# Layer 2 of a graph-attention stack: probabilities transposed in 32x32 blocks by VectorE and moved by DMA in groups of four tiles, instead of by TensorE

## The chip, the cores and the metric

The kernel runs on one core of one Trainium2 chip. The metric is the device time of one execution in microseconds. Engines are named PE (TensorE, the matrix engine; PEld is its weight load), DVE (VectorE), ACT (ScalarE), POOL (GpSimd) and SP (SyncE, which here only issues DMAs).

## What is computed

Input are 16 graphs of 1024 nodes with 64 features, and for each an adjacency matrix of 1024 x 1024 integers. Four attention layers follow one another, each as `x = layernorm(x + gnn(x, adj))`. Layer 2, which the change touches, has 8 heads:

```python
q, k, v = (x @ W + b for each)            # reshaped to 8 heads of 64
scores = einsum('bmhd,bnhd->bhmn', q, k) / sqrt(64) + edge_bias[edges]
scores = leaky_relu(scores, 0.2)
scores = where(edges > 0, scores, -1e9)
attn = softmax(scores, axis=-1)
out = einsum('bhmn,bnhd->bmhd', attn, v).reshape(b, m, 8 * 64)
return out @ Wp + bp
```

All is float32. The adjacency holds zeros and ones.

## The kernel before

The kernel loops over the 16 graphs. A tile is the block of 128 nodes (rows) by 1024 nodes (columns) of one head's attention matrix: layers 0, 1 and 3 have 8 tiles each, layer 2 has 64 (8 heads by 8 row blocks, taken as 4 pairs of heads). A step of layer 2 is the two tiles of a head pair for one row block, so layer 2 has 32 steps (`STEPS2`), eight per pair.

A tile n of layer 2 goes through these stations:

- PE, `scores`: a mask matmul (identity times mask, 2 instructions of 512 columns) and the query-key product as two float32r parts (q_hi, q_lo, 2 instructions each) into one of two PSUM slots, `score[n % 2]`. The slot is free when the leaky step of tile n-2 is done.
- ACT, `relu_part`: ReLU of the scores to `probs[n % 4]` in SBUF, line 668.
- DVE, `leaky`: combines scores and ReLU into the negated leaky ReLU with its row minimum, in place, line 926. (Another, longer branch is taken for graphs with more than one edge type.)
- ACT, `exps`: the exponential in place, with the row sum, line 679.
- PE, `turn_tile`: eight 128x128 transposes of `probs` into the PSUM area `turn`, line 384.
- DVE, `copy_tile`: copy of `turn` to `probsT[n % 4]` in SBUF, line 955.
- PE, `pv_pair`: the values product of the two tiles of a step, 8 x 2 matmuls of 128 columns (two instructions each, 32 in all), the two heads in two halves of the array's columns, into `outT`, line 412. It is done in two halves, `part` 0 and 1.

All engines have hand-written instruction orders. On PE a step s issues the scores of the first tile of step s+1, the extra work if there is any, half a values product of an earlier step, the transposes of the first tile, the scores of the second tile of step s+1, a half product again, and the transposes of the second tile. Extra work per pair of heads comes in set steps: the heads of the pair before are transposed back (`turn_out`, step 2 of a pair), the queries of the next pair (steps 3 and 4, line 456) and its values (step 5, `make_vw`, line 469). DVE does per step: leaky of n+2, copy of n, leaky of n+3, copy of n+1. ACT: exponential of n, ReLU of n+2, exponential of n+1, ReLU of n+3. `keep_clock` puts matmuls without a use where PE would idle between layers.

SP issues per graph the loads of x and of its transpose for the next graph, the eight 512 KB tiles of the next adjacency (`load_adj`; two buffers, each load from the third on waits until POOL has read the tile before, `s_adj_free`), and the store. POOL turns each adjacency tile into a mask (`convert`, lines 1177 to 1182), two per pair of heads, and between them adds the heads of each pair.

The semaphores that matter: `s_probs` (exponential done), `s_turned` and `s_turn_free` (`turn` filled and read), `s_pv` (values product done), `s_out_copied` (`outT` copied out by ACT).

Of the kernel before, what the change touches and what calls it, by code (L numbers as in the profile page):

```python
# [34 lines left out]
P = 128  # L35
# [17 lines left out]
PVS = NT // 2 * 2 + STEPS2 + NT  # L53
# [11 lines left out]
def extra_use(s):  # L65
# [7 lines left out]
    return None  # L73


def transposer_uses():
# [7 lines left out]
    for s in range(STEPS2):  # L84
        if extra_use(s):
            uses.append(extra_use(s))
        uses += [("tile", L2_0 + 2 * s), ("tile", L2_0 + 2 * s + 1)]
# [6 lines left out]
def build(nc, x, xT, adj, W0, W0T, a0T, W1, W1T, a1T, bias1, WqT, bq, WkT, bk, WvT, bv, edge_bias, Wp, bp,  # L94
# [3 lines left out]
    with ExitStack() as ctx:  # L98
# [90 lines left out]


# [22 lines left out]
        s_turned = sem("s_turned")  # L213
        s_turn_free = sem("s_turn_free")
# [45 lines left out]
        def _(sp):  # L260
# [9 lines left out]
            def load_adj(g, before):  # L270
                for t in range(NT):

                    if before is not None or t >= 2:
                        sp.wait_ge(s_adj_free, (0 if before is None else before * NT + NT) + t - 1)
                    sp.dma_start(adj_in[:, t % 2, :],
                                 adj[bass.ds(g, 1), t * P:(t + 1) * P, :].rearrange("a p j -> p (a j)")).then_inc(s_adj[t % 2], 16)

# [28 lines left out]
            load_adj(0, None)  # L306
            with sp.Fori(0, B - 1) as g:

                sp.wait_ge(s_xin_free, g + 1)
                load_x(g + 1)  # L310
                load_adj(g + 1, g)
# [3 lines left out]
            load_x(B - 1)  # L315
            store(B - 1)
# [6 lines left out]
        def _(pe):  # L323
# [75 lines left out]
            def pv_pair(g, s, part):  # L399

                pair, t = divmod(s, NT)
                n = L2_0 + 2 * s
                if part == 0:
                    if t == 0:
                        in_sbuf(pe, g, ("vw", pair))
                        pe.wait_ge(s_out_copied, g * 14 + 4 + 2 * pair)
                    if s == 0:
                        side_in_sbuf(pe, g, ("beta", 0))
                    in_sbuf(pe, g, ("tile", n + 1))
# [109 lines left out]
            with pe.Fori(0, B) as g:  # L519
# [31 lines left out]
                for s in range(STEPS2):  # L551
# [4 lines left out]
                    late = s >= 2 and t != 1  # L556
# [16 lines left out]
                    if s:  # L573
                        pv_pair(g, s - 1, 0)
                        if t == 0:
                            pv_pair(g, s - 1, 1)
# [694 lines left out]
```

## Time and profile before

| quantity | value |
|---|---|
| median of 3 runs | 10149.99 us (10137.19 to 10156.25) |
| span of the profiled execution | 10161.5 us |
| PE busy | 9662.1 us (95%) |
| DVE busy | 7780.4 us (77%) |
| ACT busy | 6859.0 us (67%) |
| POOL busy | 1409.9 us (14%) |
| mean granted PE clock | 0.988 of full |
| DMA traffic | 95.11 MB |

The profiled execution's own time is its span; the runs' times are taken without the profiler. Times in rows are microseconds from the span's start; a merged row gives start, duration, engine, line, operation, output and input, and the number of instructions. Matmuls are pipelined and their ends are modelled, so consecutive PE rows overlap by a little, and the distance of two starts is the better measure.

### The profile page before, as it was taken

The page shows a single profiled execution, that of the slowest core. Times are in us where ns is not written, and L with a number is a line of the kernel's source. Part 1 is how long each engine was busy: PE and PEld are TensorE (multiplying, and loading weights), DVE is VectorE, ACT ScalarE, POOL GpSimd, SP SyncE. Part 2 cuts the span into 40 slices and gives each one's busy share as a digit, 9 for nine tenths or more (in the row PEclk, how much of TensorE's full clock was granted, in tenths as well). Part 3 has the DMA queues.
Part 4 walks back from the last instruction along what each step waited for, and adds up shares of the span by engine and source line. Part 5 has one row for each costly group of instructions (what it writes and reads, how often), then busy time and mean ns, then how long its engine had stood idle before and what let it go on. Part 6 is the DMA issues. An engine that isn't in the chain of part 4 may idle for free.

```text
span 10161.5 us, 205999 instructions
## 1 busy us (share of the span) xinstructions
PE 9662.1 (95%) x80620; PEld 5343.6 (53%) x80620; DVE 7780.4 (77%) x11658; ACT 6859.0 (67%) x7901; POOL 1409.9 (14%) x582
## 2 busy tenths in 40 slices
PE   7999999999999999999999999999999999999999
PEld 5537355373554735547365473654736446364463
DVE  5786967869678696786967869687696876968769
ACT  4676756768567685766857668576685766857667
POOL 1203012030110301103011020111201112021000
PEclk9999999999999999999999999999999999999999
DMA  1000000000000000000000000000000000000000
GB/s 33 10 9 14 1 13 9 9 14 1 15 7 9 14 1 17 5 9 14 1 17 6 9 14 1 17 5 13 10 1 17 5 13 10 2 19 3 5 1 2
DMA packets 60304, 95.11 MB, mean 9 GB/s; under 512 B 41794, under 2 KB 41794, under 8 KB 59266
## 3 DMA queue, kind: packets, MB, share of 16 engines
q1 hardware_dynamic: 59266, 80.98, 2.6%
q8 instruction: 687, 11.26, 0.5%
q14 instruction: 351, 2.88, 0.1%
HBM read 76.77 MB, written 4.19 MB: 8 GB/s over the span
## 4 chain that ended last, share of the span: by engine, by line
issue 55%; PE 34%; DVE 4%; POOL 4%; ACT 3%; DVEq 0%; SPq 0%; POOLq 0%; DMA 0%; ACTq 0%
PE psum L384 9%; PE psum L376 8%; PE psum L412 5%; PE psum L372 4%; PE psum L456 3%; PE psum L616 2%; ACT work L668 2%; DVE work L955 2%; PE psum L469 1%; DVE q_lo L1019 1%; POOL no_edge L1179 1%; ACT q_hi L716 1%; POOL rstd L1199 1%; POOL mask_next L1182 1%; PE psum L448 1%
## 5 line engine op out<-in xcount | busy, mean ns | idle before, releaser
L825 ACT ACTIVATE work<-vw,ucol 128x1024 f32<-128x1024 f32 x3072 | 3313.8, 1141 | 484.5 <-PE psum L616 482.2
L616 PE MATMUL psum<-work,pick 128*32 128x512 f32 x32768 | 3634.7, 596 | 4.1 <-ACT work L825 3.7
L1126 DVE TENSOR_SCALAR work<-vw,ucol 128x1024 f32<-128x1024 f32 x5120 | 3446.8, 749 | 209.9 <-ACT ucol L805 116.3
L926 DVE CUSTOM_DVE_ANT_0 work<-psum,work 128x1024 f32<-128x1024 f32 x1284 | 1568.5, 1223 | 888.8 <-ACT work L668 840.1
L616 PEld LDWEIGHTS psum<-work,pick 128*32 128x32 f32 x32768 | 1014.7, 110 | 2330.3 <-issue 2229.6
L955 DVE COPY work<-psum 128x1024 f32<-128x1024 f32 x1410 | 1723.1, 1222 | 653.4 <-PE psum L384 649.0
L668 ACT ACTIVATE work<-psum,beta 128x1024 f32<-128x1024 f32 x1024 | 1142.0, 1115 | 1180.6 <-PE psum L376 1180.6
L384 PE MATMUL psum<-ident,work 128*128 128x128 f32 x11280 | 1555.7, 281 | 237.1 <-DVE work L955 95.9
L384 PEld LDWEIGHTS psum<-ident,work 128*128 128x128 f32 x11280 | 1222.6, 142 | 667.2 <-issue 505.9
L679 ACT ACTIVATE work<-work,least 128x1024 f32<-128x1024 f32 x1282 | 1463.5, 1142 | 38.9 <-DVE least L926 38.4
L412 PE MATMUL psum<-work,vw 128*64 128x128 f32 x16384 | 1064.0, 277 | 4.7 <-DVE work L955 4.7
L412 PEld LDWEIGHTS psum<-work,vw 128*64 128x64 f32 x16384 | 878.5, 137 | 291.5 <-issue 277.2
L1199 POOL TENSOR_TENSOR rstd<-rstd,neg_half 128x8 f32<-128x8 f32 x64 | 124.0, 1938 | 5480.9 <-DVE rstd L1000 5480.9
L372 PE MATMUL psum<-mask,ident_b 128*128 128x512 bf16 x2568 | 787.2, 389 | 98.9 <-issue 42.7
L376 PE MATMUL psum<-x_split,q_hi 128*128 128x512 f32 x2048 | 840.0, 491 | 0.0
L376 PE MATMUL psum<-x_split,q_lo 128*128 128x512 f32 x2048 | 646.7, 397 | 0.0
L448 PE MATMUL psum<-mask,ident_b 128*128 128x512 bf16 x2112 | 476.6, 380 | 0.0
L1210 POOL TENSOR_TENSOR za<-za,heads_T 128x512 f32<-128x512 f32 x96 | 122.8, 1279 | 2513.4 <-DVE heads_T L962 2509.6
L376 PEld LDWEIGHTS psum<-x_split,q_hi 128*128 128x128 f32 x2048 | 391.9, 191 | 149.4 <-issue 2.8
L668 ACT ACTIVATE work<-psum,sbias 128x1024 f32<-128x1024 f32 x260 | 287.6, 1112 | 251.7 <-PE psum L376 251.7
L394 PE MATMUL psum<-work,vw 128*64 128x128 f32 x6144 | 437.0, 286 | 20.4 <-DVE work L955 19.9
L394 PEld LDWEIGHTS psum<-work,vw 128*64 128x64 f32 x6144 | 341.7, 141 | 199.6 <-issue 151.0
(130 smaller groups left out, 6240.2 us busy)
## 6 DMA issues: line engine op xcount, KB each, us to landing
adj_in<-in_adj SPq DMA_DIRECT2D x128, 512.0 KB, 3.5
x_in<-in_x SPq DMA_DIRECT2D x17, 256.0 KB, 3.2
xT_in<-in_xT SPq DMA_DIRECT2D x17, 256.0 KB, 4.5
out<-yout SPq DMA_DIRECT2D x16, 256.0 KB, 2.6
work<-in_WqT SPq DMA_DIRECT2D x1, 128.0 KB
work<-in_WkT SPq DMA_DIRECT2D x1, 128.0 KB
work<-in_WvT SPq DMA_DIRECT2D x1, 128.0 KB
work<-in_Wp SPq DMA_DIRECT2D x1, 128.0 KB
```

The costliest lines, as they stand in the source:

```text
L372: pe.matmul(slot[:, cols], ident_b[:], mask[:, t, cols], start=True, stop=False)
L376: mm = pe.matmul(slot[:, cols], left, right[:, cols], start=False, stop=(k == len(parts) - 1))
L384: mm = pe.transpose(turn[:, j * P:(j + 1) * P], src[:, j * P:(j + 1) * P], ident[:])
L394: mm = pe.matmul(outT[half, t * P:(t + 1) * P], value[:, j, :], src[:, j * P:(j + 1) * P], start=(j < 2), stop=(j >= NT - 2))
L412: mm = pe.matmul(outT[F * h:F * h + F, t * P:(t + 1) * P], vw[:, pair % 2, j, F * h:F * h + F], probsT[(n + h) % 4][:, j * P:(j + 1) * P], ...
L616: mm = pe.matmul(slot[32 * q:32 * q + 32, cols], pick[:, 15 - kk:47 - kk], ring[kk % 4][q][:, cols], start=False, stop=(kk == 15), skip_gr ...
L668: act.activation(probs[n % 4], score[n % 2], ACT.Relu, bias=bias, scale=GAIN[layer]).then_inc(s_relu, 1)
L679: act.activation(probs[n % 4], probs[n % 4], ACT.Exp, bias=least[:, n % 4:n % 4 + 1], scale=-1.0, accum_out=total).then_inc(s_probs, 1)
L825: ins = act.activation(ring[kk % 4][q], v3, ACT.Relu, bias=col)
L926: dve.tensor_tensor_reduce(probs[n % 4], score[n % 2], probs[n % 4], -ALPHA[layer], 3.0e38, ALU.add, ALU.min, least[:, n % 4:n % 4 + 1]).t ...
L955: dve.tensor_copy(probsT[k], turn).then_inc(s_turn_free, 1)
L1126: ins = dve.tensor_scalar(ring[kk % 4][q], v3, col, 0.0, ALU.add, ALU.max)
```

## The change

- VectorE transposes a tile in 32x32 blocks straight from `probs` in SBUF to a group buffer `blocks[k % 2]` in SBUF (four tiles, 16 KB per partition). This leaves each block turned, but not moved to its partitions.
- A group ("quad") k is the four tiles of steps 2k and 2k+1. When its four tiles are written, SP issues 16 DMAs from `blocks` to `quadT`, each of 32 partitions, 8 runs, 512 B per run, which put block row a to block column c. `MOVED` is 15: groups 0 to 14 of 16 go this way, the last is transposed by PE as before.
- The values product takes a whole group: 256 columns per matmul, 8 x 2 matmuls, half of it in each step, `LAG` = 2 groups behind the scores.
- The next graph's adjacency loads 2 to 7 are issued between the groups' DMAs, and POOL converts 3, 3, 2 and 0 tiles in the four pairs instead of 2 each.
- Heads are transposed back in step 6 of the next pair, and `outT` is copied in two halves in steps 0 and 4.
- ScalarE's ReLU waits for VectorE's block transpose of tile n-4 in place of PE's transpose.
- Scratch of the branch for more edge types is placed elsewhere, as its buffers are now used.

```diff
+QUADS = STEPS2 // 2
+MOVED = QUADS - 1
+LAG = 2
+PV2 = NT // 2 * 2
+PVS = PV2 + QUADS + NT
...
-    if t == 2 and pair:
+    if t == 6 and pair:
         return ("heads", pair - 1)
...
+        blocks = [quad_of(8), quad_of(12)]
+        quadT = [quad_of(4), quad_of(16)]
...
+            ADJ_AFTER = {2: (2,), 3: (3,), 4: (4,), 8: (5,), 10: (6,), 11: (7,)}
+
+            def move_quads(g, more):
+
+                for k in range(MOVED):
+                    written = sp.to_reg(g * 4 * MOVED + 4 * k + 4)
+                    read = sp.to_reg(ONE + g * PVS + PV2 + k - 1) if k >= 2 else None
+                    sp.wait_ge(s_setup, SETUP)
+                    sp.wait_ge(s_blocks, written)
+                    if k >= 2:
+                        sp.wait_ge(s_pv, read)
+                    src = blocks[k % 2].rearrange("p (b c x) -> p b c x", c=4, x=P)
+                    dst = quadT[k % 2].rearrange("p (b c x) -> p b c x", c=4, x=P)
+                    for turn_ in range(4):
+                        for a in range(4):
+                            c = (a + turn_) % 4
+                            sp.dma_start(dst[32 * c:32 * c + 32, :, a, :], src[32 * a:32 * a + 32, :, c, :])\
+                              .then_inc(s_moved[k % 4], 16)
+                    if more:
+                        load_adj(g + 1, g, ADJ_AFTER.get(k, ()))
...
+            def pv_quad(g, k, part):
+
+                pair, tt = divmod(k, 4)
                 if part == 0:
-                    if t == 0:
+                    if tt == 0:
                         in_sbuf(pe, g, ("vw", pair))
...
+                    if k < MOVED:
+                        pe.wait_ge(s_moved[k % 4], g * (MOVES[k % 4] * 256) + (moved_before(k) + 1) * 256)
+                    else:
+                        in_sbuf(pe, g, ("tile", L2_0 + 4 * k + 3))
+                src = turned_quad(k).rearrange("p (b a h x) -> p b a h x", a=4, h=2, x=F)
+                cols = slice(2 * tt * P, 2 * tt * P + 2 * P)
                 for j in range(part * NT // 2, (part + 1) * NT // 2):
                     for h in range(2):
-                        mm = pe.matmul(outT[F * h:F * h + F, t * P:(t + 1) * P], vw[:, pair % 2, j, F * h:F * h + F],
-                                       probsT[(n + h) % 4][:, j * P:(j + 1) * P], start=(j == 0), stop=(j == NT - 1))
+                        dst = outT[F * h:F * h + F, cols].rearrange("p (t a i) -> p a t i", t=2, a=4)
+                        mm = pe.matmul(dst, vw[:, pair % 2, j, F * h:F * h + F],
+                                       src[:, j, :, h, :].rearrange("p a (t i) -> p a t i", t=2),
+                                       start=(j == 0), stop=(j == NT - 1))
...
-                    if late:
-                        pv_pair(g, s - 2, 1)
-                    if not extra:
+                    if s >= 2 * LAG:
+                        pv_quad(g, s // 2 - LAG, s % 2)
+                    if not in_quad(n)[3]:
                         turn_tile(g, n)
-                        if more:
-                            scores(g, n + 3)
...
+                    if more:
+                        scores(g, n + 3)
+                    if not in_quad(n)[3]:
+                        turn_tile(g, n + 1)
+                for k in range(QUADS - LAG, QUADS):
+                    pv_quad(g, k, 0)
+                    pv_quad(g, k, 1)
...
+                if n - 4 >= L2_0 and in_quad(n - 4)[3]:
+                    act.wait_ge(s_blocks, g * 4 * MOVED + n - 4 - L2_0 + 1)
...
+            def turn_tile(g, n):
+
+                k, half, h, moved = in_quad(n)
+                if k >= 2 and half == 0 and h == 0:
+                    dve.wait_ge(s_moved[(k - 2) % 4],
+                                g * (MOVES[(k - 2) % 4] * 256) + (moved_before(k - 2) + 1) * 256)
+                if moved:
+                    dve.wait_ge(s_probs, ONE + g * TILES + n + 1)
+                    dst = blocks[k % 2].rearrange("p (b h t i) -> p b h t i", h=2, t=2, i=32)
+                    dve.transpose(dst[:, :, h, half, :], probs[n % 4].rearrange("p (b j) -> p b j", j=32))\
+                       .then_inc(s_blocks, 1)
+                    return
...
-                    copy_tile(g, n)
-                    if more and not extra:
+                    turn_tile(g, n)
+                    if more:
                         leaky(g, n + 3, flagged)
-                    copy_tile(g, n + 1)
-                    if more and extra:
-                        leaky(g, n + 3, flagged)
+                    turn_tile(g, n + 1)
...
-                        for t in (2 * pair, 2 * pair + 1):
+                        for t in ((0, 1, 2), (3, 4, 5), (6, 7), ())[pair]:
```

## Rows read from the trace of the kernel before

**Rows 1.** Timeline of PE: start, us, engine, line, operation; layer 2's beginning and end.
```profile
3322.61 1.01 PE L372 MATMUL psum<-mask,ident_b 128*128 128x512 bf16 x2
...
3327.92 0.67 PE L372 MATMUL psum<-mask,ident_b 128*128 128x512 bf16 x2
...
3573.62 1.14 PE L422 MATMUL psum<-ident,heads_T 128*128 128x128 f32 x8 [0.70 <-ACT heads_T L696]
```

**Rows 2.** Busy time of a window inside layer 2: PE, PEld, DVE, ACT, POOL, clock, DMA.
```profile
3388.00:3451.00 63.00, 61.43 (x518) 46.35 (x516) 42.07 (x52) 40.20 (x54) 21.37 (x8) 1.00 0.05 18
```

**Rows 3.** Timeline of PE, a steady tile of layer 2.
```profile
3443.36 1.09 PE L412 MATMUL psum<-work,vw 128*64 128x128 f32 x16
3444.39 1.09 PE L384 MATMUL psum<-ident,work 128*128 128x128 f32 x8
3445.32 0.59 PE L372 MATMUL psum<-mask,ident_b 128*128 128x512 bf16 x2
...
3446.77 1.09 PE L412 MATMUL psum<-work,vw 128*64 128x128 f32 x16
```

**Rows 4.** Timeline of DVE and ACT in steady tiles, with idle time before.
```profile
3452.70 1.22 DVE L955 COPY work<-psum 128x1024 f32<-128x1024 f32 x1
3454.97 1.23 DVE L926 CUSTOM_DVE_ANT_0 work<-psum,work 128x1024 f32<-128x1024 f32 x1 [1.04 <-ACT work L668]
...
3453.71 1.12 ACT L668 ACTIVATE work<-psum,beta 128x1024 f32<-128x1024 f32 x1 [1.17 <-PE psum L376]
```

**Rows 5.** Groups by line, 3325 to 3572: busy, mean ns, idle before and its releaser.
```profile
L955 DVE COPY work<-psum 128x1024 f32<-128x1024 f32 x64 | 78.2, 1222 | 35.4 <-PE psum L384 35.4
L668 ACT ACTIVATE work<-psum,beta 128x1024 f32<-128x1024 f32 x64 | 71.4, 1115 | 75.3 <-PE psum L376 75.3
```

**Rows 6.** Timeline of PE: a whole values product of two tiles, and what follows.
```profile
3394.14 1.97 PE L412 MATMUL psum<-work,vw 128*64 128x128 f32 x32
3396.03 1.09 PE L384 MATMUL psum<-ident,work 128*128 128x128 f32 x8
```

**Rows 7.** The page's costliest groups: layer 3's DVE operation from SBUF to SBUF.
```profile
L1126 DVE TENSOR_SCALAR work<-vw,ucol 128x1024 f32<-128x1024 f32 x5120 | 3446.8, 749 | 209.9 <-ACT ucol L805 116.3
```

**Rows 8.** SP issues: start and us in the timeline; ns min/median/max by line.
```profile
4.55 0.65 SPq L264 DMA_DIRECT2D work<-in_WqT  x1
...
L267 SPq DMA_DIRECT2D x_in<-in_x x17: 383/384/434, 15.3 to 9549.1; - x17
...
L268 SPq DMA_DIRECT2D xT_in<-in_xT x17: 532/547/591, 15.8 to 9549.5; - x17
```

**Rows 9.** The page's DMA issues: count, KB each, us from issue to landing.
```profile
xT_in<-in_xT SPq DMA_DIRECT2D x17, 256.0 KB, 4.5
out<-yout SPq DMA_DIRECT2D x16, 256.0 KB, 2.6
```

**Rows 10.** Windows of the store and of an adjacency load: last columns are DMA share, GB/s.
```profile
3234.00:3238.50 4.50, 3.90 (x28) 3.01 (x28) 1.87 (x3) 1.96 (x4) 0.00 (x0) 0.79 0.27 62
...
3263.00:3264.00 1.00, 0.02 (x1) 0.05 (x2) 0.59 (x2) 0.00 (x0) 0.38 (x1) 1.00 0.99 356
```

**Rows 11.** Groups by line: the longest operation of POOL's convert, three per tile.
```profile
L1177 POOL TENSOR_SCALAR mask_next<-adj_in 128x1024 bf16<-128x1024 int32 x120 | 436.5, 3638 | 16.2 <-POOL mask_next L1182 11.2
```

**Rows 12.** Timeline of PE: the extra work of a pair, queries and values.
```profile
3412.57 1.98 PE L456 MATMUL psum<-xTa,Aq 65*128 65x512 f32 x4
...
3431.21 2.05 PE L469 MATMUL psum<-Cv,xTa 65*128 65x128 f32 x16
```

**Rows 13.** Windows of 3.4 us: after the length PE busy; the third last is the clock.
```profile
3224.90:3228.30 3.40, 1.26 (x9) 0.86 (x8) 3.13 (x7) 2.69 (x4) 0.00 (x0) 1.00 0.04 10
3228.30:3231.70 3.40, 1.50 (x4) 0.81 (x4) 3.26 (x19) 0.60 (x2) 1.42 (x1) 0.62 0.02 5
3332.00:3335.40 3.40, 2.25 (x15) 1.62 (x14) 3.12 (x6) 2.58 (x5) 1.86 (x1) 1.00 0.45 154
3335.40:3338.80 3.40, 3.21 (x18) 2.16 (x17) 2.17 (x4) 2.24 (x3) 0.00 (x0) 1.00 0.00 0
```

More of the change, by code:

```diff
@@ L73, in extra_use, with in_quad, moved_before @@
     return None
+def in_quad(n):
+    s, h = divmod(n - L2_0, 2)
+    k, half = divmod(s, 2)
+    return k, half, h, k < MOVED
+def moved_before(k):
+    return len(range(k % 4, k, 4))
+MOVES = tuple(len(range(r, MOVED, 4)) for r in range(4))
 def transposer_uses():
@@ L86, in transposer_uses @@
             uses.append(extra_use(s))
-        uses += [("tile", L2_0 + 2 * s), ("tile", L2_0 + 2 * s + 1)]
+        uses += [("tile", n) for n in (L2_0 + 2 * s, L2_0 + 2 * s + 1) if not in_quad(n)[3]]
     uses += [("heads", HP - 1), ("xT", 2), ("v3", 0)]
@@ L188, in build, with quad_of, turned_quad @@
         v3 = vw[:, 0, :, :].rearrange("p a b -> p (a b)")
+        def quad_of(first):
+            return work[:, first:first + 4, :].rearrange("p a b -> p (a b)")
+        blocks = [quad_of(8), quad_of(12)]
+        quadT = [quad_of(4), quad_of(16)]
+        def turned_quad(k):
+            return quadT[k % 2] if k < MOVED else blocks[k % 2]
         s_load = sem("s_load")
@@ L213, in build @@
         s_turned = sem("s_turned")
+        s_blocks = sem("s_blocks")
+        s_moved = [sem(f"s_moved{i}") for i in range(4)]
         s_turn_free = sem("s_turn_free")
@@ L315, in _ @@
             load_x(B - 1)
+            move_quads(B - 1, False)
             store(B - 1)
@@ L555, in _ @@
                     extra = extra_use(s)
-                    late = s >= 2 and t != 1
                     if more:
@@ L795, in _ @@
                     if t == 0 and pair:
-                        copy_out(g, 1 + pair, NT + s)
-                copy_out(g, 1 + HP, NT + STEPS2)
+                        copy_out(g, 1 + pair, PV2 + 4 * pair - 2, (0,))
+                    if t == 4 and pair:
+                        copy_out(g, 1 + pair, PV2 + 4 * pair, (1,))
+                copy_out(g, 1 + HP, PV2 + QUADS - 2, (0,))
+                copy_out(g, 1 + HP, PV2 + QUADS, (1,))
                 x_turned(g, 2)
@@ L932, in leaky @@
                 head = 2 * pair + h
-                scaled, part = work[:, 8, :], work[:, 9, :]
+                scaled, part = probs[n % 4], zb[:].rearrange("p t f -> p (t f)")
                 ready = dve.to_reg(g * L3_0 + n + 1)
@@ L938, in leaky @@
                 for k in range(2, TYPES):
-                    typed(dve.tensor_scalar(part, mask[:, t, :], k * CODE, delta[:, k, head:head + 1], ALU.is_equal,
-                                            ALU.mult))
-                    typed(dve.tensor_tensor(scaled, scaled, part, ALU.add))
-                typed(dve.scalar_tensor_tensor(out=part, in0=scaled, scalar=ALPHA[2], in1=scaled, op0=ALU.mult,
+                    for cols in (slice(0, HALF), slice(HALF, N)):
+                        typed(dve.tensor_scalar(part, mask[:, t, cols], k * CODE, delta[:, k, head:head + 1],
+                                                ALU.is_equal, ALU.mult))
+                        typed(dve.tensor_tensor(scaled[:, cols], scaled[:, cols], part, ALU.add))
+                typed(dve.scalar_tensor_tensor(out=scaled, in0=scaled, scalar=ALPHA[2], in1=scaled, op0=ALU.mult,
                                                op1=ALU.max))
-                dve.tensor_tensor_reduce(probs[n % 4], part, part, -0.5 / GAIN[2], 3.0e38, ALU.add, ALU.min,
+                dve.tensor_tensor_reduce(scaled, scaled, scaled, -0.5 / GAIN[2], 3.0e38, ALU.add, ALU.min,
                                          least[:, n % 4:n % 4 + 1]).then_inc(s_leaky, 1)
+            def turn_tile(g, n):
[9 more added lines that the diff above has]
+                    return
+                filled(g, ("tile", n))
+                dst = turned_quad(k).rearrange("p (b a h t i) -> p b a h t i", a=4, h=2, t=2, i=32)
+                dve.tensor_copy(dst[:, :, :, h, half, :], turn.rearrange("p (b a i) -> p b a i", a=4, i=32))\
+                   .then_inc(s_turn_free, 1)
             def copy_tile(g, n):
```

51 lines of the change are left out of this document (21 added, 30 removed).

## The prediction, made before the changed kernel was built or run

> **What bounds the kernel now.** I read the stages of one graph first (busy time per window), then TensorE's timeline inside layer 2, then the same stretch on VectorE and ScalarE, then the waits grouped by line. One graph takes about 635 us (the span over 16). Layer 2 runs from its first scores at 3322.61 to the transpose of the last pair's heads at 3573.62, 251.0 us [rows 1]. In its middle the windows show PE busy 61.4 of 63 us, VectorE 42.1, ScalarE 40.2 [rows 2]: TensorE bounds this stage. A steady tile repeats every 3.41 us on PE (3443.36 to 3446.77): values product 1.03, eight transposes 0.93, scores 1.45, with no idle mark [rows 3]. VectorE spends 1.15 on the leaky step and 1.15 on the copy out of PSUM (start to start), then idles 1.04; ScalarE idles 1.17 [rows 4]. Over the stage the idle time of both ends on TensorE's scores or transposes [rows 5]. So taking transposes off PE can shorten this stage, and only this stage; the other 384 us of a graph stay as they are.
>
> **What goes.** 60 of 64 tiles per graph lose their PE transposes: 60 x 0.93 = 56 us of PE time per graph, 893 us in all. The last group of four keeps them. The values product keeps its columns: 4 x 0.95 = 3.8 us per group of four tiles (32 instructions in 1.90 us per two tiles [rows 6]); 256 columns per matmul instead of 128 halve the instruction count. I bound that between -1.9 us (if the time went by instruction) and, for the strided source and the 32-column runs in PSUM, +3.8 (each column at half pace), and take 0: source and result keep contiguous runs of 64 and 32 values.
>
> **What comes on VectorE.** A 32x32-block transpose of 128x1024 from SBUF to SBUF in place of the copy from PSUM. No row has it. Bounds: 0.75 us (the fastest SBUF to SBUF 1024-column operation [rows 7]) to 2.3 (two passes of the copy). I take the copy's 1.15, the nearest in columns and type. VectorE then needs 2.3 per tile, 9.2 per group of four, below what follows.
>
> **What comes on SP and the DMA queues.** Each of 15 groups per graph issues 16 DMAs of 128 KB (32 partitions x 8 runs of 512 B), 3840 in all, on SP alone. Issue price: the 128-partition x load, the one with most runs, costs 0.38 us, loads on 64 partitions 0.55 to 0.65 [rows 8]. The new ones have 32 partitions, so I go by the latter, 0.66 from start to start (bounds 0.43 and 0.9: the 128-partition price, and one more step as large as that from 128 to 64). Landing: 2.6 for the store and 4.5 for a read of 256 KB [rows 9]; for 128 KB inside SBUF I take 2.4 (1.8 to 4). From the last block written to a usable group: D = 0.1 + 15 x 0.66 + 2.4 = 12.4 us. Transfers: the store ran 256 B packets at share 0.27 and 62 GB/s, so about 230 GB/s if always busy; the adjacency reads about 356 at share 0.99 [rows 10]. A group's 2.1 MB takes 6 to 9 us at that, under the 10.6 of issue, so it adds nothing here.
> The Trainium skill (SBUF — State Buffer, "Door 1: The DMA port swizzle") speaks against this: how many of the 16 ports the partitions reach sets the bandwidth, and 32 adjacent partitions reach 8. No row here shows it; an estimate by that page's 436 GB/s halved is 9.6 us a group, still under the issue time, but without the margin.
> SP's other work: the adjacency loads of the next graph are put behind groups 2, 3, 4, 8, 10 and 11. Each waits for GpSimd, whose convert is three operations, the longest 3.6 us [rows 11]; by the schedule below each awaited convert is over before its load's turn, so I cost them at nothing (behind a late one all later moves would queue, 16 at a time). Register moves ahead of the waits run while SP is idle.
>
> **The cycle.** Group k is multiplied in steps 2k+4 and 2k+5 (a step is two tiles). Let E be PE's end of step 2k+1. The last tile's path behind it is ReLU 1.1, leaky 1.15, transpose 1.15 and handoffs: blocks complete at E + 3.5. They land at E + 3.5 + D. From there PE does half a product 1.9, scores 1.46, scores 1.46, the other half 1.9, scores 1.46 = 8.2 us, and that ends step 2k+5, two groups later. So two periods are 3.5 + D + 8.2, P = (D + 11.7)/2 = 12.05 us, against PE's own work of 4 x 1.46 + 3.8 = 9.65: the waits on the DMAs, about 2.4 us per group, take the place of the wait on TensorE. Before, four tiles took 13.65 plus the extras.
>
> **Sum for one graph.** Fill: the first scores to the end of the two starting tiles stay 5.3 us [rows 1]; steps 0 to 3 have no product and go at VectorE's 4.6 plus handoffs, 4.9 each, plus 1.2 for the query split in step 3: 20.8. Group 0's blocks are ready at 5.3 + 9.8 + 3.5 = 18.6, landed at 31.0, and PE is there at 26.1 + 3.4 = 29.5: wait 1.5. Then 13 periods (steps 4 to 29) at 12.05: 156.7. Extras (queries 1.9, values 2.0 [rows 12], heads 1.0, eight transposes like a tile's): those in even steps lie inside the wait; five in odd steps count half, 4.9. Clock: 3.4 us with PE busy for only 1.26 were followed by a granted clock of 0.62, 3.4 us with 2.25 busy by 1.00 [rows 13]. The waits of 2.4 lie between; 3.4 us at the 1.2 GHz level instead of 2.4 cost 1.7, and I count 0.5 per group, 6.5. Tail: from step 30 on 3.5 + D + 7.6 for the two last groups + 0.7 = 24.2; this part was short before because only one and a half pairs were left. Total 26.1 + 1.5 + 156.7 + 4.9 + 6.5 + 24.2 = 219.9, against 251.0: 31.1 us less per graph, 498 us in 16. The profiled execution's span is 10161.5, the median 10149.99, 0.1% apart; the saving is 4.9% of either, and from the median it gives 9652 us.
> D counts 6.5 times in the 13 periods, once in the tail and once in the first wait: each us of D is 8.5 us per graph, 136 us in all. At D = 16 nothing is left.
>
> **Rivals.**
> (a) Cheap issue: at 0.43, D = 0.1 + 6.45 + 2.2 = 8.8, and PE's work bounds again, with extras 11.1 per group: 26.1 + 144.3 + 20.5 = 191, 60 us per graph less, 9190 us. For it: the 128-partition rows. Against it: the 64-partition ones. 0.15.
> (b) Slower than before: the 16 DMAs of a group take 17 us to land, by an issue price of 0.9 or because a 32-partition transfer runs at half the rate of [rows 10], 115 to 178 GB/s, 12 to 18 us per group. Then P = 14.35, and 26.1 + 6 + 13 x (14.35 + 1.4) + 28.7 = 266, 15 us per graph more, 10,380 us. It decides from D = 16. For it: many packets of 512 B, no such transfer in the trace. 0.22.
> (c) The clock: if each wait drops it and a group's 8.2 us of PE work behind it lose 1.7 us or more, P grows by about 1.2 beyond what is counted: 13 x 1.2 = 15.6, half of the gain given back, 9900 us. 0.15.
> (d) The strided product at half pace: PE's work per group 13.4, P = 13.95, + 31 per graph: about 10,150 us, no change. 0.08, shared by the same and the slower side.
> By the Trainium skill (SBUF — State Buffer, the note on cachelines under "Door 1: The DMA port swizzle") any non-contiguous PSUM pattern slows matmuls much; that is rival (d). Runs of 32 values here are contiguous, and no row shows such a pattern.
> (e) Forecast: waits of some 2 us per group on the moved blocks, 0.40. That the change does not take effect can nearly be excluded: the trace has no instruction of the branch for flagged graphs, and the unflagged one turns 60 tiles as described.
>
> **Numbers.** 9652 us. The range takes in (a) nearly and (b) up to its own price: 9230 to 10,350, with about 0.08 left out below and 0.12 above. About 0.2% (20 us) is what a measurement of this kernel can tell from no change. Faster by more: 0.40 + 0.15 + 0.15 = 0.70; same 0.06; slower 0.24.
>
> **What would show it.** In layer 2's steady stretch PE should show idle time before the product, released by the moved DMAs, of 1 to 4 us per group, a group every 12 to 13 us; SP's 16 issues should span about 10 us; VectorE's transpose 1.2 us. No idle before the product and a group per 11 us is (a); a group per 15 or more is (b), and issue durations against landing times tell which half; granted clock under 0.9 through layer 2 is (c); product instructions of twice the length are (d). Most likely to be wrong: the issue price, then the landing.

## The result and the profile after

The changed kernel takes 9713.61 us (9705.1 to 9722.03) against 10151.01 for the kernel before on the same chip: ratio 0.9568, 95% interval 0.9554 to 0.9581. The forecast was 9652 in a range of 9230 to 10,350. 437 us were saved where 498 were expected. One execution of all those below, of the kernel with four moves on ScalarE's queue, was in a slow state (14,790.52 us at a granted clock of 0.553, against 10,025 to 10,041 for its other three), and it counts in that kernel's median alone.

The page of after (engine, busy us, share, instructions; the moving queue; the chain that ended last; groups by line; landing):

```profile
PE 8693.8 (90%) x64203; PEld 4229.6 (44%) x64748; DVE 7718.4 (79%) x11658; ACT 6774.4 (70%) x7901; POOL 1410.6 (15%) x582
...
q1 hardware_dynamic: 1103746, 584.54, 25.5%
...
issue 59%; PE 16%; SPq 11%; DVE 5%; ACT 4%; DMA 3%; POOL 2%; DVEq 0%; ACTq 0%; POOLq 0%
...
L477 PE MATMUL psum<-work,vw 128*64 128x256 f32 x8192 | 1105.8, 419 | 403.9 <-DMA work<-work 403.7
L1020 DVE STREAM_TRANSPOSE work<-work 128x1024 f32<-128x1024 f32 x960 | 1190.5, 1240 | 40.0 <-DMA work<-work 38.9
...
work<-work SPq DMA_DIRECT2D x3840, 128.0 KB, 2.4
```

PE lost 968 us of busy time, but 404 us came back as idle time before the values product (L477), nearly all of it released by the moved DMAs. Nothing of that kind stood on the page of before. SP's queue, at 0% of the chain of work that ended last before, is now 11% of it. VectorE's busy time hardly changed: 960 block transposes took the place of 960 copies. 404 us are 1.7 a group, within the 1 to 4 that the forecast had named as its sign.

PE's timeline in the same graph as [rows 1]: layer 2's first scores, the first half products of groups 0 to 4, the last of the 16 groups, the transpose of the heads. The bracket is the idle time before the row and what ended it.

```profile
3171.11 0.59 PE L431 MATMUL psum<-mask,ident_b 128*128 128x512 bf16 x2
...
3199.69 2.70 PE L477 MATMUL psum<-work,vw 128*64 128x256 f32 x16 [3.42 <-DMA work<-work]
...
3212.51 1.95 PE L477 MATMUL psum<-work,vw 128*64 128x256 f32 x16
...
3227.30 3.68 PE L477 MATMUL psum<-work,vw 128*64 128x256 f32 x16 [4.97 <-DMA work<-work]
...
3240.15 1.95 PE L477 MATMUL psum<-work,vw 128*64 128x256 f32 x16 [0.37 <-DMA work<-work]
...
3387.90 8.81 PE L477 MATMUL psum<-work,vw 128*64 128x256 f32 x64 [2.55 <-DMA work<-work]
...
3396.64 1.41 PE L488 MATMUL psum<-ident,heads_T 128*128 128x128 f32 x8
```

Layer 2 takes 3396.64 - 3171.11 = 225.5 us against 251.0; one graph earlier it is 222.0 (2570.56 to 2792.54) against 250.2. So 25.5 and 28.2 us saved, and the spans (10161.5 and 9713.2) give 28.0 a graph on average. Outside layer 2, from the heads' transpose to the next layer 2, the time moved from 380.4 to 379.5 us: the change lives in the stage where it was put. The span is 225.5 = 28.6 to the first product, 173.1 for 13 groups (13.3 each, from 3199.69 to group 13's 3372.79), 23.85 for the rest.

The timeline of SP's queue, the moves of three groups and more (start, time over all issues, count):

```profile
3187.35 38.09 SPq L328 DMA_DIRECT2D work<-work  x48
3225.77 0.34 SPq L309 DMA_DIRECT2D adj_in<-in_adj  x1
3226.32 10.95 SPq L328 DMA_DIRECT2D work<-work  x16
3237.58 0.34 SPq L309 DMA_DIRECT2D adj_in<-in_adj  x1
3241.70 10.49 SPq L328 DMA_DIRECT2D work<-work  x16
...
3332.33 11.60 SPq L328 DMA_DIRECT2D work<-work  x16
```

The sixteen issues of a group begin when VectorE has written its last block, at 3241.70, and the product of that group starts at 3253.98: D = 12.3 us. The adjacency load behind a group costs SP 0.34 us. Below, D is compared between kernels as (time of a group's issues) - (one issue) + (median landing): here 10.49 - 0.62 + 2.4 = 12.3.

That is the D of the groups with an even number. In those with an odd one, an issue among the fourth to seventh takes about 1 us longer, so that the sixteen take 11.3 to 11.7 us on average (10.95 and 11.60 in the rows above). From the first issue to the last landing, all 240 groups average 12.8. It is so with half of the bytes too (10.3 and 10.9 to 11.5), so full transfers are not the reason. Of the 122 issues in after that take over 0.25 us more than the median, 115 have a 16 KB packet of the queue that the page names instruction (q8) between 1.5 us before and 0.2 us after them, with half of the bytes 111 of 112; of the 3718 other issues in after it is 158. In the group that starts at 3253.75 the fifth issue takes 1.55 us, and the DMA queues from 3253.7 to 3258.2 show:

```profile
q8 instruction: 1, 0.02, 1.4%
```

That is a coincidence in time; no run here changes it, so that the packet is the cause is not shown.

### The profile page after: what moved, and what is told of

Its sections match the earlier page's. It is cut to its first block, busy times and chain, and to the rows that moved or that the text cites. A ratio compares the mean times of both kernels' runs of the same rounds, so it can differ in the third digit from the quotient of the medians.

```text
span 9713.2 us, 176082 instructions
## 1 busy us (share of the span) xinstructions
PE 8693.8 (90%) x64203; PEld 4229.6 (44%) x64748; DVE 7718.4 (79%) x11658; ACT 6774.4 (70%) x7901; POOL 1410.6 (15%) x582
## 3 DMA queue, kind: packets, MB, share of 16 engines
q1 hardware_dynamic: 1103746, 584.54, 25.5%
## 4 chain that ended last, share of the span: by engine, by line
issue 59%; PE 16%; SPq 11%; DVE 5%; ACT 4%; DMA 3%; POOL 2%; DVEq 0%; ACTq 0%; POOLq 0%
SPq L328 11%; PE psum L477 4%; PE psum L435 3%; DMA work<-work 3%; ACT work L728 2%; DVE work L1020 2%; PE psum L674 2%; PE psum L431 2%; DVE work L989 1%; PE psum L522 1%; PE psum L443 1%; POOL rstd L1279 1%; ACT work L739 1%; PE psum L514 1%; PE psum L453 1%
## 5 line engine op out<-in xcount | busy, mean ns | idle before, releaser
L674 PE MATMUL psum<-work,pick 128*32 128x512 f32 x32768 | 3623.5, 594 | 12.1 <-ACT work L888 12.1
L477 PE MATMUL psum<-work,vw 128*64 128x256 f32 x8192 | 1105.8, 419 | 403.9 <-DMA work<-work 403.7
L1020 DVE STREAM_TRANSPOSE work<-work 128x1024 f32<-128x1024 f32 x960 | 1190.5, 1240 | 40.0 <-DMA work<-work 38.9
L477 PEld LDWEIGHTS psum<-work,vw 128*64 128x64 f32 x8192 | 617.0, 148 | 841.7 <-issue 364.6
L431 PE MATMUL psum<-mask,ident_b 128*128 128x512 bf16 x2231 | 734.5, 400 | 261.5 <-DVE least L989 164.6
L435 PE MATMUL psum<-x_split,q_hi 128*128 128x512 f32 x2048 | 855.3, 499 | 0.0
L443 PE MATMUL psum<-ident,work 128*128 128x128 f32 x3600 | 500.0, 283 | 167.6 <-ACT work L739 80.9
L435 PE MATMUL psum<-x_split,q_lo 128*128 128x512 f32 x2048 | 648.4, 398 | 0.0
L1257 POOL TENSOR_SCALAR mask_next<-adj_in 128x1024 bf16<-128x1024 int32 x120 | 436.5, 3638 | 1164.5 <-DMA adj_in<-in_adj 1156.4
L443 PEld LDWEIGHTS psum<-ident,work 128*128 128x128 f32 x3600 | 393.1, 142 | 362.3 <-issue 305.4
L1037 DVE COPY work<-psum 128x1024 f32<-128x1024 f32 x386 | 470.8, 1220 | 84.6 <-PE psum L443 81.5
L435 PEld LDWEIGHTS psum<-x_split,q_hi 128*128 128x128 f32 x2048 | 403.5, 197 | 161.2 <-issue 18.7
L514 PE MATMUL psum<-mask,ident_b 128*128 128x512 bf16 x2032 | 459.5, 380 | 6.3 <-issue 3.0
L453 PE MATMUL psum<-work,vw 128*64 128x128 f32 x6144 | 434.6, 285 | 29.3 <-DVE work L1037 29.3
```

The source lines that it names most:

```text
L431: pe.matmul(slot[:, cols], ident_b[:], mask[:, t, cols], start=True, stop=False)
L435: mm = pe.matmul(slot[:, cols], left, right[:, cols], start=False, stop=(k == len(parts) - 1))
L443: mm = pe.transpose(turn[:, j * P:(j + 1) * P], src[:, j * P:(j + 1) * P], ident[:])
L477: mm = pe.matmul(dst, vw[:, pair % 2, j, F * h:F * h + F], src[:, j, :, h, :].rearrange("p a (t i) -> p a t i", t=2), start=(j == 0), stop ...
L674: mm = pe.matmul(slot[32 * q:32 * q + 32, cols], pick[:, 15 - kk:47 - kk], ring[kk % 4][q][:, cols], start=False, stop=(kk == 15), skip_gr ...
L1020: dve.transpose(dst[:, :, h, half, :], probs[n % 4].rearrange("p (b j) -> p b j", j=32))\
```

## The experiments

Ratios are to the kernel before, on the same chip. Two questions were open: what in the moves sets D (the count of issues, their bytes, or the partitions they reach), and what else is on the path. The expectations call some kernels by short names: e3 has 8 DMAs over 64 partitions, e5 the new order on VectorE, e6 and e7 that order and 2 or 4 moves on ScalarE's queue.

**Half of the bytes, half of the DMAs.**

```diff
# half of the bytes
-dst[32 * c:32 * c + 32, :, a, :], src[32 * a:32 * a + 32, :, c, :]
+dst[32 * c:32 * c + 32, 0:4, a, :], src[32 * a:32 * a + 32, 0:4, c, :]
# half of the DMAs
-for turn_ in range(4):
+for turn_ in range(2):
```

> The changed kernel with its 16 DMAs per group each moving 4 of the 8 runs, so 64 KB instead of 128 KB (half of the moved probabilities stay behind, so layer 2's output is not the reference's). Theory: a group's time from written to usable, D, is 16 issues of 0.66 us on SP's queue plus one landing of 2.4; bytes don't count. Then nothing moves: 9700 us within 30, 16 issues still span 10 to 10.6 us. Rival, transfers: if D is set by the bytes or by 32 partitions reaching few ports, D falls from 12.3 towards 7 and the time to about 9150 us.

> The changed kernel with only the first 8 of a group's 16 DMAs (the other half of the blocks is not moved, so layer 2's output is not the reference's). Theory: D falls to 0.1 + 7 x 0.66 + 2.4 = 7.1 us, under the 7.6 at which TensorE's own work fills the period; the wait before the product vanishes, a group takes 11.1 us with extras instead of 13.3, the granted clock in layer 2 rises to 0.98 or more, layer 2 takes about 189 us instead of 225.5, and the kernel about 9130 us (9080 to 9250). Rival: if something else of the new order holds the groups at 13 us (VectorE's order, ScalarE, the product's strided operands), it stays above 9500.

Half of the bytes: 9661.43 (0.9507, 0.9488 to 0.9526), 52 us less than after. Half of the DMAs: 9204.21 (0.9057, 0.9039 to 0.9075), 509 less. The line of the moves with half of the bytes (ns min/median/max of an issue, then us to landing):

```profile
L328 SPq DMA_DIRECT2D work<-work x3840: 585/601/2137, 182.0 to 9351.5; - x192
...
DMA to landing us min/median/max: 2.0/2.0/4.0
```

The same line with half of the DMAs, and who waited for them:

```profile
L328 SPq DMA_DIRECT2D work<-work x1920: 585/617/1928, 181.5 to 8885.6; - x192
...
  PEld psum L477: 11.2, 29
  PE psum L477: 0.2, 1
...
DMA to landing us min/median/max: 2.3/2.4/3.9
```

An issue costs the same, 0.60 to 0.62 us, with 64 KB as with 128 KB. With eight DMAs a group, PE no longer waits for them (0.2 us in the run), and what is left is near the forecast's rival (a), 9190, which stood for PE's own work being the bound. The forecast gave each us of D a price of 136 us. Half of the bytes lowers D by 0.6 (table below), which is 84 us by that price; 52 came, and 9661 is 39 below the expectation's 9700, which allowed 30.

**Half of the DMAs, all of the bytes, over 64 and then 128 partitions.** The count falls to 8, of 256 KB each.

```diff
# 64 partitions, turn_ in range(4), a in range(2)
-dst[32 * c:32 * c + 32, :, a, :], src[32 * a:32 * a + 32, :, c, :]
+dst[64 * c:64 * c + 64, :, 2 * (turn_ // 2) + a, :], src[64 * a:64 * a + 64, :, 2 * (turn_ // 2) + c, :]
# 128 partitions, turn_ in range(2), a in range(4)
-dst[32 * c:32 * c + 32, :, a, :], src[32 * a:32 * a + 32, :, c, :]
+dst[:, 4 * turn_:4 * turn_ + 4, a, :], src[:, 4 * turn_:4 * turn_ + 4, a, :]
```

> The changed kernel with 8 DMAs of 64 partitions and 256 KB per group in place of 16 of 32 partitions and 128 KB: the same bytes, half the issues (blocks land at the wrong partitions, so layer 2's output is not the reference's). Theory, count of issues: as with half the DMAs, 9130 us plus up to 60 for a landing 0.4 us longer. Rival, bytes: D stays above 11 and the time near 9650.

> Eight DMAs a group instead of sixteen, each of all 128 partitions and four runs (256 KB each), so that the bytes of a group stay as they are, 2.1 MB, and the count is halved as with eight DMAs of 64 partitions (9694.8). The blocks stay on their own partitions, so the products read rows in the wrong place and the output is not the reference's; what is computed, and how much, is the same. Theory A (the count of issues sets the step, and with it a second limit that belongs to moving 32 or 64 adjacent partitions, 35.9 to 42.7 ns a packet against 29.2 over 128): the issue stays near 0.65 us, the last of 8 is issued after 5.2 us and landed after about 8, so D falls from 12.3 to about 8 us, as with half of the DMAs (9204), and the run comes to 9200 to 9350. Theory B (the queue takes a time per byte or per row of the descriptor, whatever its shape): the issue grows to about 1 to 1.3 us, 8 issues span 8 to 10.5 us as with 64 partitions, and the run stays at 9650 to 9720.

64 partitions: 9694.84 (0.954, 0.9521 to 0.9559), a plain miss: halving the count gave 19 us. 128 partitions: 9295.15 (0.9156, 0.9139 to 0.9174), 418 less than after. The line of the moves over 64 partitions:

```profile
L328 SPq DMA_DIRECT2D work<-work x1920: 590/993/2502, 179.6 to 9392.3; - x192
...
DMA to landing us min/median/max: 3.2/5.0/9.0
```

The line of the eight moves over 128 partitions:

```profile
L327 SPq DMA_DIRECT2D work<-work x1920: 593/692/1710, 180.8 to 8977.9; - x192
...
DMA to landing us min/median/max: 2.6/3.6/4.8
```

Over 64 partitions the queue itself slows: 0.99 us an issue, and 5.0 to land, and a group's issues take 8.54 and 7.84 us in two groups, 8.2 on average, so that D = 8.2 - 1.0 + 5.0 = 12.2 is where it was. Over 128 the same bytes by the same count need 6.31 - 0.69 + 3.6 = 9.2, where theory A had about 8. So there is a second limit behind the count of issues, and it goes by partitions. A rival would be that the moves over 128 leave every byte on its partition, while the others cross. But of the eight over 64 half stay too (`c` equal to `a`), and they land no closer behind the one before (1.23 to 1.31 us, medians by place in the group) than those that cross (1.18 to 1.30); over 128 it is 0.88 to 0.93.

**Sixteen DMAs over 128 partitions; the order of the halves.** The first keeps count and bytes and changes only the partitions (`dst[:, 2 * turn_:2 * turn_ + 2, a, :]`); the second sends a in the order 0, 2, 1, 3.

> The changed kernel with its 16 DMAs of 128 KB per group each over all 128 partitions with 2 runs of 512 B, in place of 32 partitions with 8 runs: same bytes, same number of runs and DMAs (nothing changes partition, so layer 2's output is not the reference's). Theory A, partitions: 32 or 64 adjacent partitions reach only part of SBUF's ports, which held e3 at about 10 us for 2.1 MB and stretched the issues of e7; over 128 partitions the transfers take 7 us or less, and the issue costs 0.40 to 0.45 as in the loads on 128 partitions; D falls to about 9 and the time to 9200 us (9130 to 9300). Theory B, packets: 4096 runs of 512 B per group take that time by themselves whatever the partitions; landing and D stay at 11 or more, and the time at 9600 or more.

> The changed kernel with the source groups of a turn in the order 0, 2, 1, 3 in place of 0, 1, 2, 3, so that neighbours in the queue read and write different halves of the 128 partitions; nothing else. Theory A (ports): neighbouring DMAs overlap better, landing falls from 2.4 and the stretched issues (up to 2.1 us) get rarer: 20 to 80 us less than 9714. Theory B (packets), or engines that never run two DMAs at once: the same within 15.

9697.69 (0.9545, 0.9525 to 0.9566) and 9717.43 (0.9563, 0.9546 to 0.958): neither is worth anything alone, and both intervals overlap that of after. The first has the time of theory B without its reason: the same packets went faster in the kernel with 8 DMAs over 128 partitions, and what held this one was the issue, 0.62 us and not the 0.40 to 0.45 of the expectation. What the engines move shows in windows of some us while a group moves (the last two columns are the DMA share and GB/s; a share over 1 is more than one packet in flight). The windows are chosen so that no bytes of an adjacency load, which would count, fall into them. After, 16 DMAs over 32 partitions:

```profile
3243.00:3251.00 8.00, 7.84 (x40) 4.57 (x40) 6.72 (x8) 6.25 (x8) 0.00 (x0) 1.00 0.87 198
```

8 DMAs over 64 partitions:

```profile
3250.00:3258.00 8.00, 7.84 (x37) 4.50 (x37) 6.83 (x9) 6.85 (x11) 0.00 (x0) 1.00 1.12 219
```

8 DMAs over 128 partitions:

```profile
3104.00:3110.00 6.00, 6.00 (x32) 3.39 (x32) 5.49 (x8) 5.29 (x7) 0.00 (x0) 1.00 1.01 287
```

16 DMAs over 128 partitions:

```profile
3252.50:3261.00 8.50, 8.50 (x41) 4.99 (x41) 7.04 (x9) 7.12 (x9) 0.00 (x0) 1.00 0.68 196
```

The first and the last are the pace of the issues (131,072 B each 0.66 us are 198 GB/s), at 0.87 and 0.68 of the engines' time. At a full share the first would move 228, an estimate; two queues that push over 32 partitions reached 203 to 207 (below). Eight DMAs over 64 partitions move 219 with the engines full, eight over 128 move 287. A group's 2.1 MB then needs 9.2 to 10.3 us over 32 partitions, 9.6 over 64 and 7.3 over 128. Sixteen issues need 10.5. So after stands at two limits that nearly coincide: the issues bound it, and the transfers would just below. Taking one away alone (8 DMAs of 64 partitions; 16 of 128) gives 16 to 19 us, no more than the noise can hide; taking both gives 418. These runs follow roughly from D, at 136 us per us away from after's 12.27, half of the bytes with 32 us between:

| kernel | D | by D | measured |
|---|---|---|---|
| after | 12.3 | - | 9713.6 |
| half of the bytes | 10.25 - 0.60 + 2.0 = 11.65 | 9629 | 9661.4 |
| 8 of 64 partitions | 8.2 - 1.0 + 5.0 = 12.2 | 9704 | 9694.8 |
| 16 of 128 partitions | 10.56 - 0.62 + 2.2 = 12.1 | 9696 | 9697.7 |
| 8 of 128 partitions | 6.31 - 0.69 + 3.6 = 9.2 | 9299 | 9295.2 |
| half of the DMAs | 5.21 - 0.62 + 2.4 = 7.0 | 8996 | 9204.2 |

The last is beyond the point at which D stops to count, since PE's work is then the longer; by the same line its 9204 us would belong to a D of 8.5. With the averages of all groups in place of the D above (12.8 for after; 12.1, 12.7, 12.6, 9.5 and 7.2 in the table's order) the picture is the same.

**The clock.** Eight matmuls without a use stand before the product's wait, once the score slot is free.

```diff
+if k < MOVED and k < QUADS - LAG:
+    slot_free(g, L2_0 + 4 * (k + LAG) + 3)
+    for _ in range(KEEP_QUAD):
+        pe.matmul(score[1][:, 0:HALF], ident_b[:], mask[:, 0, 0:HALF], start=True, stop=True)
```

> The changed kernel with eight more matmuls without a use (0.22 us each, 1.8 us together) on TensorE before it waits for a moved group. Theory: part of what the prediction missed is the granted clock, 0.92 to 0.96 in layer 2, which falls to the 1.2 GHz level after the longer waits (a half product then took 3.68 us instead of 1.95). With the wait partly filled the clock stays at 0.98 or more there and the period loses 0.4 to 0.7 us: 9590 us (9550 to 9650). Rival: the filling delays the groups whose wait is shorter than 1.8 us by as much as the clock gives back: 9700 within 30, or slower.

9729.95 (0.9573, 0.9557 to 0.9589): no gain, though the mean granted clock rose from 0.972 to 0.988. Its timeline shows why this can't decide what the clock costs:

```profile
3235.11 1.90 PE L472 MATMUL psum<-mask,ident_b 128*128 128x512 bf16 x8 [0.90 <-DVE least L994]
3236.93 1.95 PE L482 MATMUL psum<-work,vw 128*64 128x256 f32 x16
```

The half product runs at full pace (1.95 instead of 3.68) without a wait of its own, but 1.8 us of filler stand before it and themselves wait for VectorE. What the products got back, the filler took. How much PE time the clock cost in after can be read from the products, the same 8192 instructions in each kernel. Busy us and mean ns with half of the DMAs, where PE hardly waits:

```profile
L477 PE MATMUL psum<-work,vw 128*64 128x256 f32 x8192 | 987.8, 385 | 0.4 <-DMA work<-work 0.2
```

After has 1105.8 us there, 118 more; with the filler it is 991.2. What those 118 us are worth in the run's time stays open.

**VectorE's order.** The block transpose of tile n+1 is placed ahead of the leaky step of n+3.

```diff
 turn_tile(g, n)
+early = in_quad(n)[3]
+if early:
+    turn_tile(g, n + 1)
 if more:
     leaky(g, n + 3, flagged)
-turn_tile(g, n + 1)
+if not early:
+    turn_tile(g, n + 1)
```

> The changed kernel with one edit on VectorE: in every step of a moved group the block transpose of tile n+1 comes ahead of the leaky step of tile n+3, so a group is complete right after its last exponential and not 3.5 us behind TensorE's end of the step. Theory: the period is half of (path to the last block + D + TensorE's 8.2 and its lost clock); taking 3.3 us from the path takes 1.65 from each of 13 periods until the next limit, SP's 16 issues and the adjacency load (about 11.1 us) or TensorE's work with extras (11.1). 9350 us (9280 to 9450). Rival: the period is already bound by a throughput, SP's issues or the transfers, and the chain only looks like it: then no gain over 20 us, 9690 or more. Second rival: the leaky step comes later, TensorE's slots are freed later, and it gets slower than 9714.

9508.09 (0.9359, 0.9344 to 0.9375): 206 us less than after, though 158 above the expectation. In after the last transpose of a group queues behind leaky steps with which VectorE catches up after it idled 5.47 us:

```profile
3233.99 1.22 DVE L989 CUSTOM_DVE_ANT_0 work<-psum,work 128x1024 f32<-128x1024 f32 x1 [5.47 <-ACT work L728]
...
3239.28 1.19 DVE L989 CUSTOM_DVE_ANT_0 work<-psum,work 128x1024 f32<-128x1024 f32 x1
...
3240.39 1.24 DVE L1020 STREAM_TRANSPOSE work<-work 128x1024 f32<-128x1024 f32 x1
```

One leaky step, 1.1 us, leaves the path of two periods. Part of the gain is also the clock's, as the waits got shorter: the products, 1105.8 us in after, are busy 70 us less:

```profile
L477 PE MATMUL psum<-work,vw 128*64 128x256 f32 x8192 | 1036.1, 399 | 255.0 <-DMA work<-work 254.8
```

The rest of the hoped gain was largely stopped by SP's queue. Over these four groups, 11.5 us each, it waits for VectorE for 1.9 us in all (SP's timeline; in four groups of after from 3253.75 it waited 7.1):

```profile
3183.31 46.06 SPq L328 DMA_DIRECT2D work<-work  x64
```

**Some of the moves on ScalarE's queue.** On top of that order, the last 2, then the last 4, of each 16 DMAs are issued by ScalarE (`ON_ACT`), between the exponential and the ReLU; then the four with the order 0, 2, 1, 3.

> As e5, and the last 2 of a group's 16 DMAs issued by ScalarE, behind its exponential of the next even step. Theory: SP's issues fall from 10.6 to 9.2 us, D by up to 1.3; if issue is what holds e5, 9250 to 9330; if the transfers hold it (2.1 MB took about 10 us with half the issues in e3), no gain beyond 30 us over e5. Rival: ScalarE's 1.2 us per group in front of its ReLU delay the scores' slots, and it is slower than e5.

> As e6 with 4 of the 16 DMAs on ScalarE: SP's issues fall to 7.9 us, ScalarE's work per group rises by 2.5 to about 12.5 with its extras. If issue bounds e5 and e6, another 50 to 100 us less than e6; if transfers bound, the same as e6 within 30; if ScalarE's queue bounds, slower than e6 by 100 or more.

> e7 (two issuing queues, block transposes first) with the order 0, 2, 1, 3. In e7 SP's 12 issues took 10.3 us instead of 7.9, so the transfers held both queues. Theory A: with neighbours on different halves the 12 issues take 8 to 9 us and the time falls by 200 us or more, to 9800 or less. Theory B: no change from 10037 within 40.

Two: 9406.88 (0.9261, 0.9246 to 0.9277), the fastest kernel here that does the whole work. Four: 10,036.53 (0.9877, 0.9857 to 0.9897), 630 slower than two. Four in the other order: 9928.36 (0.9772, 0.975 to 0.9794), 108 less. The kernel with two gained 101 us, between what its expectation gave for issues (9250 to 9330) and for transfers (at most 30), which fits that both held it. SP's timeline in the kernel with four:

```profile
3331.13 10.20 SPq L331 DMA_DIRECT2D work<-work  x12
```

ScalarE's in the same stretch, its own issues (ACTq) among its work:

```profile
3331.17 0.59 ACTq L760 DMA_DIRECT2D work<-work  x1
3331.32 0.19 ACT L742 ACTIVATION_READ_ACCUMULATOR work<-work,least 128x1 f32 x1
3331.79 3.07 ACTq L760 DMA_DIRECT2D work<-work  x3
3335.05 1.11 ACT L731 ACTIVATE work<-psum,beta 128x1024 f32<-128x1024 f32 x1 [3.54 <-issue]
```

Twelve issues take SP 10.20 us, hardly less than sixteen did (10.49): 0.85 each. While they ran, two windows show 203 and 207 GB/s at a share of 0.90 and 0.91, and the order of the halves tells that partitions set this rate. The order 0, 1, 2, 3, then 0, 2, 1, 3:

```profile
3348.00:3356.00 8.00, 5.74 (x20) 2.89 (x16) 5.18 (x7) 5.38 (x7) 0.00 (x0) 0.84 0.90 203
...
3372.00:3379.00 7.00, 3.30 (x11) 2.13 (x10) 3.57 (x5) 4.37 (x6) 0.00 (x0) 0.73 1.03 226
```

With neighbours in the queue on different halves of the partitions, SP's twelve issues take 9.7 us on average over all groups instead of 10.5, and the run 108 us less: more than theory B's 40, less than theory A's 200. With one queue, where issues were the limit, the same order gave nothing (9717). ScalarE's three issues hold up its ReLU by 3.54 us, and 496 us of such waits stand in the whole run, with 656 us of PE waiting for VectorE's leaky step behind it, while PE waits only 0.9 us for the moves. With two DMAs it is 316 us (2.3 at most) and 218, and SP's 14 issues need 10.1 us on average instead of 10.9 for 16.

**The first and last two groups on TensorE.** On top of the kernel with two, groups 0, 1, 14 and 15 are transposed by PE, so that fill and tail have no D in them.

```diff
+MOVED_SET = tuple(range(2, 14))
-    return k, half, h, k < MOVED
+    return k, half, h, k in MOVED_SET
+if k >= 2 and half == 0 and h == 0 and k - 2 not in MOVED_SET:
+    dve.wait_ge(s_pv, ONE + g * PVS + PV2 + k - 1)
```

> e6 with groups 0 and 1 and the last two (14, 15) of a graph transposed by TensorE, 12 of 16 moved. In the first four steps TensorE has about 2 us per step to spare, and at the end it waits for group 14. Theory: the wait of 3.4 us before the first product and the 2.6 us before group 14 go, some 5 to 7 us per graph: 9310 us (9270 to 9370) against e6's 9407. Rival: TensorE's transposes of 8 more tiles cost 7.4 us per graph where it was not idle: 9400 or more.

9841.2 (0.9688, 0.9671 to 0.9705): a miss by sign, 434 slower than without. The last added line is one reason, which the timeline shows. Group 2's blocks go to the buffer that the product of group 0 reads, so VectorE waits for that product (171 us in the whole run, 32 times):

```profile
3273.20 2.37 DVE L1047 STREAM_TRANSPOSE work<-work 128x1024 f32<-128x1024 f32 x2 [7.85 <-PE psum L489]
...
3288.09 2.37 DVE L1047 STREAM_TRANSPOSE work<-work 128x1024 f32<-128x1024 f32 x2 [3.60 <-PE psum L489]
```

And the fill grew: first scores 3224.96, first product 3262.96, 38.0 us instead of the 28.6 of after, as PE's eight transposes wait for the copies and the queries share `turn` with them. How much of the 434 us lies in each is not separated.

## Why the prediction was right, point by point

- **Issue price.** Forecast 0.66 from start to start; measured 0.617 and the gap, 10.49 / 16 = 0.66. Right in size, wrong in reason. I took it from the loads on 64 partitions [rows 8], as if fewer partitions cost more. Over 128 partitions the same moves cost 0.62 too, while the x load costs 0.41 over 128 in the same run. What the price follows in place of partitions was not found; not bytes (0.60 with half of them).
- **Landing and D.** 2.4 and 12.4 forecast; 2.4 and 12.3 measured in even groups, 12.8 on average over all, as one issue of each odd group is longer. Nothing in the forecast stood for that.
- **Transfers behind the issue.** "Under the 10.6 of issue, so it adds nothing" held for after, where the issues set the pace. But it was read as a fair margin, and the runs with 64 partitions and with two queues show that there is next to none. The Trainium skill (SBUF — State Buffer, "Door 1: The DMA port swizzle") gives 32 adjacent partitions half of the ports, and 64 adjacent ones no more; by its figure that is 218 GB/s, an estimate of 9.6 us a group. The window over 64 partitions agrees, with 219; over 32 no run shows a full share from one queue, and 203 to 207 came from two. Over all 128 the runs show 287 and not twice as much, so here the step is 1.3.
- **VectorE's transpose.** 1.15 forecast, between bounds of 0.75 and 2.3; 3240.39 to 3241.56 with the leaky step behind it, 1.17.
- **The strided product.** Cost 0 forecast, rival (d) otherwise. A half product is 1.88 us from start to start (3212.51 to 3214.39), as before. The Trainium skill (SBUF — State Buffer, the note on cachelines under "Door 1: The DMA port swizzle") says that non-contiguous PSUM patterns slow matmuls significantly; for the runs of 32 values here, 1.88 us against 1.9, it does not hold.
- **The period.** 12.05 and extras 0.4 and clock 0.5 made 12.9 a group; measured 13.3. The terms of one pair of periods, 3227.30 to 3253.98: PE 10.2 (forecast 8.2), the last tile's path 4.2 (3.5), D 12.3 (12.4). The term that failed is PE's 8.2: the half product behind the wait took 3.68 instead of 1.9, at a granted clock of 0.80 in these 10.2 us. I had counted 0.5 us a group for the clock, which is less than this pair lost (1.8, so 0.9 a group). Over the whole run, products and scores (L477, L431, L435) are busy 154 us longer than with half of the DMAs, an estimate of 0.7 a group for the clock. So the cause was named and its size too small. The 0.7 on the tile's path is VectorE's catching up; the experiment with its order took it and the leaky step off together, so its own share is not shown.
- **Fill and tail.** 31.0 and 20.8 forecast (the tail from the product of group 13), 28.6 and 23.85 measured: the first 2.4 too long, the second 3.1 too short. That they nearly cancel is luck. The sum is 219.9 against 225.5, in the graph before 222.0.
- **GpSimd's masks and the adjacency loads.** Cost nothing forecast. Behind a group's moves the load is issued 0.3 us after the last one (3226.32 + 10.95, then 3237.58), so no wait for GpSimd held SP there; after the first graph's loads SP never waits at that line (L309).
- **The sensitivity.** 136 us for each us of D was the most useful line of the forecast: it gives 9299 for 8 DMAs over 128 partitions, and 9295 was measured. A hit within 4 us is partly luck, as the line misses half of the bytes by 32 and leaves the clock out. By it and the measured 9714 nothing is left at D = 12.3 + (10,151 - 9714) / 136 = 15.5; the forecast said 16.

Rival (b), slower, needed an issue of 0.9 or half the rate. Neither price came in after, but 8 DMAs of 64 partitions had an issue of 0.99, and with four DMAs on ScalarE's queue 0.8: the price was there to be met, had the work been cut otherwise.

## What to carry to other kernels

A move between partitions by DMA is priced by the time from the last byte written to the last byte landed, and here that was mostly a count of issues on one queue. Before halving the count or adding a queue, work out the second limit from the windows (GB/s at a full share, in a stretch with no other transfer): where it lies close to the first (here 9.2 to 10.3 us against 10.5), one change alone shows nothing, as three of these runs show (8 DMAs of 64 partitions, 16 of 128, the other order). The same change can pay once the other limit is gone, as the order did with two queues (108 us). And when work is taken off the bounding engine, look at who sits in front of the new wait on the next engine: swapping two operations of VectorE gave 206 us, nearly half of the whole change.

## What the hardware showed that I had not expected

- A DMA's issue costs its queue 0.60 to 0.62 us with 64 or 128 KB and over 32 or 128 partitions, but grows when transfers back up: a median of 0.69 (8 of 128 partitions, 287 GB/s) and 0.99 (8 of 64 partitions, 219 GB/s), and 0.85 on average in the group shown (12 on SP, 4 on ScalarE). When most issues of a group are long, that is then a sign of full transfers. A single long one is not: each odd group has one of about 1 us more, with half of the bytes too, and nearly all of these have a 16 KB packet of the instruction queue beside them.
- The rate of transfers within SBUF depends on the partitions: 203 to 207 GB/s over 32 adjacent with two queues, 226 with neighbours in the queue on different halves, 219 over 64, 287 over 128.
- DMA issues on ScalarE cost 0.61 us (median) with two a group and 0.80 with four (2.54 at most), and they hold its own work: its ReLU waited 316 us behind them in the run with two, 496 with four.
